# Moving the transposes of y and the sum of z within the step of a pipelined attention and feed-forward kernel

## The reference

```python
normed = rms_norm(x, gamma)
q, k, v = heads of normed @ w_q, normed @ w_kv          # 8 heads of 16
q, k = taylor(q / 4), taylor(k)                         # [1, x, x (x) x / sqrt(2)]
out = (q @ (k^T v)) / max(q . sum(k), 1e-5)
x = layernorm(x + out @ w_out)
h = silu((x @ w1.T) * s1) * ((x @ w2.T) * s2)           # 128 -> 512
h = gelu((h @ h1.T) * sh1)                              # 512 -> 512
h = gelu((h @ h2.T) * sh2)
x = layernorm(x + (h @ w3.T) * s3)                      # 512 -> 128
```

## Time and profile before

| | before |
|---|---|
| median of 3 runs | 554.48 us (554.03 to 554.76) |
| profiled execution | 553.77 us, span 551.7 us |
| busy share of the span | TensorE 97%, VectorE 83%, ScalarE 82%, GpSimd 37% |
| mean granted TensorE clock | 0.996 of full |

### The profile page before, as it was taken

How to read it: one execution, slowest core, us unless ns; L and a number is a source line. 1 busy time by engine, 2 the same in 40 slices (tenths; PEclk the granted TensorE clock), 3 DMA queues, 4 the chain that set the end, 5 groups by cost and what they waited for, 6 DMA issues and landing times.

```text
span 551.7 us, 11595 instructions
## 1 busy us (share of the span) xinstructions
PE 533.3 (97%) x3578; PEld 404.2 (73%) x3578; DVE 457.1 (83%) x966; ACT 454.6 (82%) x941; POOL 202.3 (37%) x280
## 2 busy tenths in 40 slices
PE   6879999999999999999999999999999999999995
PEld 4556868878686887878788787877868687786774
DVE  5888869798797879978797987978889797888674
ACT  3777898988889888888988888898888889787774
POOL 3865334252443423345342533434144353310001
PEclk9999999999999999999999999999999999999998
DMA  8202200201211020121202112110211210010001
GB/s 288 67 23 58 58 21 7 71 21 39 58 38 57 16 55 24 38 57 38 57 0 60 35 38 57 38 57 5 52 38 38 57 38 19 1 33 6 8 13 38
DMA packets 28405, 23.81 MB, mean 43 GB/s; under 512 B 3552, under 2 KB 21472, under 8 KB 28384
## 3 DMA queue, kind: packets, MB, share of 16 engines
q1 hardware_dynamic: 28096, 23.43, 15.9%
q10 hardware_dynamic: 288, 0.10, 0.1%
HBM read 19.31 MB, written 4.22 MB: 43 GB/s over the span
## 4 chain that ended last, share of the span: by engine, by line
PE 88%; DVE 1%; ACT 1%; issue 0%; POOLq 0%; POOL 0%; DVEq 0%
PE fps L524 29%; PE fps L527 29%; PE ring L459 6%; PE ring L437 5%; PE ring L490 5%; PE ring L408 4%; PE ring L499 3%; PE ring L507 2%; PE ring L416 2%; PE fps L569 1%; PE fps L515 1%; PE ring L446 1%; PE ring L470 1%; DVE h L1113 1%; PE ring L477 0%; DVE hid_lo L1119 0%
## 5 line engine op out<-in xcount | busy, mean ns | idle before, releaser
L524 PE MATMUL fps<-hid_hi,w_hi 128*128 128x512 f32 (+1 forms) x584 | 230.6, 396 | 0.0
L527 PE MATMUL fps<-hid_lo,w_hi 128*128 128x512 f32 (+1 forms) x584 | 227.5, 391 | 0.9 <-DVE hid_lo L1127 0.5
L862 ACT ACTIVATE hid_hi<-fps,col 128x512 fp32r<-128x512 f32 x127 | 89.6, 706 | 46.9 <-PE fps L527 46.9
L524 PEld LDWEIGHTS fps<-hid_hi,w_hi 128*128 128x128 f32 x584 | 109.9, 188 | 24.9 <-issue 3.4
L527 PEld LDWEIGHTS fps<-hid_lo,w_hi 128*128 128x128 f32 x584 | 109.9, 188 | 23.4 <-DVE hid_lo L1127 0.9
L1127 DVE TENSOR_TENSOR hid_lo<-fps,hid_hi 128x512 fp32r<-128x512 f32 x127 | 86.1, 687 | 20.5 <-ACT fps L864 19.5
L864 ACT ACTIVATE fps<-fps,col 128x512 f32<-128x512 f32 x127 | 85.9, 676 | 0.0
L1113 DVE SCALAR_TENSOR_TENSOR h<-fps,col,gate_zo 128x512 f32<-128x512 f32 x64 | 47.6, 745 | 41.3 <-ACT gate_zo L849 35.9
L809 ACT ACTIVATE phiT<-ring 128x512 f32<-128x512 f32 x127 | 77.2, 637 | 3.0 <-PE ring L437 1.8
L303 DVE TENSOR_TENSOR phi_k<-phi_k 128x896 f32<-128x896 f32 x64 | 69.3, 1086 | 0.2 <-ACT v_one L792 0.2
L1119 DVE TENSOR_TENSOR hid_lo<-h,hid_hi 128x512 fp32r<-128x512 f32 x64 | 54.7, 855 | 7.9 <-ACT hid_hi L854 6.4
(11 more groups left out here) (141 smaller groups left out, 921.2 us busy)
## 6 DMA issues: line engine op xcount, KB each, us to landing
x_res<-in_x SPq DMA_DIRECT2D x16, 256.0 KB, 3.8
x_nrm<-in_x SPq DMA_DIRECT2D x15, 256.0 KB, 2.8
out<-gate_zo SPq DMA_DIRECT2D x15, 256.0 KB, 2.3
x_cols<-in_xT SPq DMA_DIRECT2D x14, 256.0 KB, 2.6
rn_row<-rn_rows SPq DMA_DIRECT2D x14, 256.0 KB, 4.2
w_raw<-in_h SPq DMA_DIRECT2D x2, 1024.0 KB, 8.8
w_raw<-in_w SPq DMA_DIRECT2D x3, 256.0 KB, 4.4
sel_raw<-in_sel SPq DMA_DIRECT2D x1, 320.0 KB, 5.1
```

The costliest lines, as they stand in the source:

```text
L524: nc.tensor.matmul(out, w[:, o:o + P], hi, start=start, stop=False)
L527: return nc.tensor.matmul(out, w[:, o:o + P], lo, start=False, stop=stop)
L862: nc.scalar.activation(hid[1 - layer][0][:, m, :], fps[:, bank, :], ACT.Gelu, scale=scale)\
```

## The change

`transpose_y` moves from behind `apply_rest` to behind `transpose_rest`, on TensorE. Its output goes to bank 2 of `ring` in place of bank 0 of `fps`, so the entry yT moves from the table FPS to RING and its semaphores with it. `sum_z` is cut in two: the addition of x1, which reads the PSUM bank, goes between gate_mult(1) and gate_lo(0) on VectorE; mean and variance stay behind `normalise` as `var_of_z`. The last step's own form is moved in the text alone. All arithmetic is the same. The change's name also says that the state is done by tiles; the diff has no edit to `state`, and it stands as before.

```diff
--- before.py
+++ after.py
@@ -42,13 +42,13 @@
 
 
 RING = (
-    ("stateT", MIDDLE, 0), ("restT", MIDDLE, 1), ("xT", FRONT, 2), ("acc0", MIDDLE, 0), ("acc1", MIDDLE, 1),
+    ("stateT", MIDDLE, 0), ("restT", MIDDLE, 1), ("xT", FRONT, 2), ("yT", TAIL, 2), ("acc0", MIDDLE, 0), ("acc1", MIDDLE, 1),
     ("kv0", FRONT, 3), ("kv1", FRONT, 2), ("kv2", FRONT, 3), ("kv3", FRONT, 2), ("qT", FRONT, 0), ("out", MIDDLE, 1),
     ("sq0", FRONT, 2), ("sq1", FRONT, 1), ("rest0", FRONT, 3), ("sq2", FRONT, 0), ("sq3", FRONT, 2), ("sq4", FRONT, 1),
     ("rest1", FRONT, 3), ("sq5", FRONT, 0), ("sq6", FRONT, 2), ("state", FRONT, 1), ("sq7", FRONT, 3))
 FPS = (
     ("a0", FFN, 0), ("b0", FFN, 1), ("a1", FFN, 2), ("b1", FFN, 3), ("a2", FFN, 0), ("b2", FFN, 1), ("a3", FFN, 2),
-    ("b3", FFN, 3), ("yT", TAIL, 0), ("two0", FFN, 1), ("two1", FFN, 2), ("two2", FFN, 3), ("two3", FFN, 0),
+    ("b3", FFN, 3), ("two0", FFN, 1), ("two1", FFN, 2), ("two2", FFN, 3), ("two3", FFN, 0),
     ("three0", FFN, 1), ("three1", FFN, 3), ("three2", FFN, 2), ("x1T", MIDDLE, 0), ("three3", FFN, 1), ("y", FFN, 3))
 
 
@@ -564,11 +564,11 @@
             def transpose_y(t):
 
                 pe.wait_ge(f_free[bank_of(FPS, "y")], read(FPS, t - 1, "y"))
-                bank_wait(FPS, f_free, t, "yT")
+                bank_wait(RING, ring_free, t, "yT")
                 for j in range(NT):
-                    mm = nc.tensor.transpose(fps[:, bank_of(FPS, "yT"), j * P:(j + 1) * P], yT[:, j * P:(j + 1) * P],
+                    mm = nc.tensor.transpose(ring[:, bank_of(RING, "yT"), j * P:(j + 1) * P], yT[:, j * P:(j + 1) * P],
                                              ident)
-                mm.then_inc(f_full, 1)
+                mm.then_inc(ring_full, 1)
 
             def last_layers(t, in_full):
 
@@ -630,6 +630,10 @@
                     if middle:
                         transpose_state(t)
                         transpose_rest(t)
+                    if is_step(t, B + 2):
+                        last_transposes()
+                    elif tail:
+                        transpose_y(t)
                     if is_step(t, 0):
                         transpose_x(0)
                     if ffn:
@@ -638,10 +642,6 @@
                     if middle:
                         apply_main(t)
                         apply_rest(t)
-                    if is_step(t, B + 2):
-                        last_transposes()
-                    elif tail:
-                        transpose_y(t)
                     if front:
                         project_kv(t, 0)
                         project_kv(t, 1)
@@ -1078,14 +1078,17 @@
                 nc.vector.tensor_scalar(veps[:, :], mv[:, :, 1], LN_EPS, None, ALU.add).then_inc(veps_ready, 1)
 
             def sum_z(t, par):
-                bank = bank_of(FPS, "yT")
+                bank = bank_of(RING, "yT")
                 if is_positive(t - 3):
                     dve.wait_ge(out_ready, t - 3)
-                dve.wait_ge(f_full, written(FPS, t, "yT"))
+                dve.wait_ge(ring_full, written(RING, t, "yT"))
                 nc.vector.tensor_tensor(z[:, :, :].rearrange("p j d -> p (j d)"),
-                                        x1[par][:, :, :].rearrange("p j d -> p (j d)"), fps[:, bank, :],
-                                        ALU.add).then_inc(f_free[bank], 1)
-                dve.wait_ge(f_free[bank], read(FPS, t, "yT"))
+                                        x1[par][:, :, :].rearrange("p j d -> p (j d)"), ring[:, bank, :],
+                                        ALU.add).then_inc(ring_free[bank], 1)
+
+            def var_of_z(t):
+                bank = bank_of(RING, "yT")
+                dve.wait_ge(ring_free[bank], read(RING, t, "yT"))
                 for j in range(NT):
                     nc.vector.bn_stats(zstats[:, j, :], z[:, j, :])
                 dve.drain()
@@ -1166,6 +1169,8 @@
 
                     gate_mult(t, 0)
                     gate_mult(t, 1)
+                if tail:
+                    sum_z(t, 1 - par)
                 if ffn:
                     gate_lo(t, 0)
                     gate_mult(t, 2)
@@ -1176,7 +1181,7 @@
                 if middle:
                     normalise(t)
                 if tail:
-                    sum_z(t, 1 - par)
+                    var_of_z(t)
                 if front and not is_step(t, B - 1):
                     sum_squares(t + 1)
                 if ffn:
```

## The result

The changed kernel takes 558.56 us (median of 6 runs, 557.96 to 560.78) against 554.62 for the one before (median of 6, measured beside it): ratio 1.0078, 95% interval 1.0062 to 1.0094. That is 3.9 us slower where 1.3 were forecast, and above the range. The profiled execution took 559.12 us for a span of 556.9.

What follows compares the result with a forecast made beforehand. TensorE's stream was taken to bound steps 3 to 16, and VectorE's gates step 17. The transposes' +0.7 us over 14 steps and sum_z's +0.6 in step 17 made +1.3: 555.8 us, range 554.1 to 556.9.

Steps and rivals of the forecast that it cites:

- So there are two regimes: Steps 3 to 16 cost slots in TensorE's stream; in step 17 nothing else covers the gates and TensorE waits for VectorE.
- 0.7 + 0.6: The sum: +0.7 us for the transposes in steps 3 to 16, +0.6 for sum_z in step 17.
- a wait in the gates of every step: Rival: silu(2) or gate_lo slips past its cover, or project_kv(1) waits for sum_z; 559.3 us, chance 0.06.
- The new place of the transposes: Behind transpose_state and transpose_rest on TensorE: four transposes take 0.44 us a step, without a wait.
- The old place: Behind apply_rest: 0.58 us of transposes leave, project_kv's first product exposes 0.20, so 0.38 to 0.39 a step is freed.
- Rival (a): Steps come out even: project_kv's load exposes only 0.14 us; only step 17's +0.6 is left, 555.1 us; chance 0.25.
- (b): Rival, faster: the load of w_qkv behind apply_rest is fetched early and hidden; 553.1 us, chance 0.07.
- The sum of the steps: Transposes' move in steps 3 to 16: 0.44 - 0.39 = +0.05 us a step, 14 steps, +0.7 us.
- The sum of z between the gates: On VectorE, 0.65 us at either place: 0 in steps 3 to 16, where cover absorbs it; not free in step 17.
- Step 17: sum_z ahead of gate_lo(0) delays each later gate by 0.60 to 0.65 us, and TensorE at two0: +0.6 us.

Runs made afterwards that it cites:

- run 2: Kernel before, with 250 instructions more in TensorE's branch that is not taken: 557.57 us (1.0062).
- run 1: Changed kernel, with 8 instructions more in TensorE's branch that is not taken: 555.31 us (1.0021).
- the late sum: In step 17 alone, sum of z in its old place behind the last gate_lo; by itself in the changed kernel: 557.62 us (1.0069).
- run 7: Changed kernel, with 4 instructions more in the branch that is not taken: 555.38 us (1.0022).
- run 5: Changed kernel, with 8 instructions more in the branch not taken and step 17's sum of z in its old place: 555.19 us (1.0021).
- run 11: Changed kernel, with the body that runs directly behind TensorE's branch and step 17's sum of z in its old place: 554.65 us (1.0017).
- run 8: Kernel before, with 226 instructions more in the branch that is not taken: 555.28 us (1.0018).
- run 4: Changed kernel, with the body that runs placed first, directly behind TensorE's branch: 555.64 us (1.0027).
- run 9: Changed kernel, with 2 instructions more in the branch that is not taken: 559.22 us (1.0082).
- Run 10: Kernel before, with the body that runs placed first, directly behind TensorE's branch: 554.54 us (1.0008).
- run 3: Changed kernel, with step 17's sum of z in its old place behind the last gate_lo: 557.62 us (1.0069).

## Why the prediction was wrong

**The step that failed** is "So there are two regimes", and with it the sum "0.7 + 0.6": it has terms for steps 3 to 17 alone, and takes all ahead of step 3 as untouched, because the code that runs there is the same. What runs is the same; where it lies is not. That is worth 1.0062 made in the kernel before (run 2, 3.4 us), and 1.0078 - 1.0021 = 0.0057, 3.2 us, taken off the changed kernel (run 1). By the rows the two profiled executions are 4.2 us apart at the transposes of step 2 (L477 49.31 and 45.07), and their spans are 5.2 apart: in this pair nothing took it back. The medians show less. One wait that can take a part back is TensorE's for GpSimd in step 2, 0.3 to 0.7 us in the four profiles with a stall and 0.6 to 1.4 in the nine without. None of the rivals was this one: "a wait in the gates of every step" gives nearly the measured time, 559.3, by a mechanism that did not happen.

There was a sign of it in the trace of the kernel before. L507's idle time of 1.12 us was put down to VectorE's att, in VectorE's timeline

```profile
30.18 0.71 DVE L1050 STREAM_TRANSPOSE att<-wide 128x512 f32<-128x512 f32 x1
```

but att was ready at 30.89 (30.18 + 0.71) and L507 began at 31.71. The last 0.8 us are the branch's: in the nine profiles with the jump and a record ahead of the edge, L507 begins 1.57 to 1.65 us behind the end of the first transfer of instructions. I read waits only from 60 us on, and so never met a branch.

**The new place of the transposes**: right to 0.01 us. The chain of waits of the changed kernel, step 8, answers to the earlier trace rows:

```profile
243.81 0.22 PE ring L470 x2
244.03 0.11 PE ring L477
244.14 0.44 PE ring L569 x4
...
248.28 1.02 PE ring L499 x8
249.29 0.94 PE ring L408 x6
```

0.44 for the four. **The old place**: project_kv's six products take 0.94 instead of 0.73, 0.21 exposed behind the tiled stage where 0.20 was taken from the load behind the state. Rival (a), that only 0.14 would be, fell, and so did (b). By the Trainium skill (TensorEngine Tiling, Key Properties) a change of tiling mode drains TensorE. The trace agrees that both followers come late, and shows that the price differs with the follower: 0.14 for a float32 transpose, 0.21 for a load of rounded weights.

**The sum of the steps** was mis-sized: the pieces say +0.06 to 0.07 a step, 0.8 to 1.0 in all, but the distances between the groups of transposes grew from a mean of 32.346 to 32.367 us, 0.02 a step. From project_out of step 2 to the first transposes of the last step (L600) it is 486.6 to 486.7 us in the five profiles with the old order (before: 544.73 - 58.01) and 487.5 to 487.6 in the five with the new one (after: 549.93 - 62.35), and 487.1 in the three with the late sum. So 0.5 us is step 17 and 0.4 the steps, where 0.7 was forecast. Why the slots of the other products are together 0.03 to 0.04 us a step shorter stays open.

**The sum of z between the gates**: in full steps free, as said. VectorE's timeline in step 8 answers to the earlier trace rows:

```profile
244.37 0.75 DVE L1116 SCALAR_TENSOR_TENSOR h<-fps,col,gate_zo 128x512 f32<-128x512 f32 x1 [0.31 <-ACT gate_zo L849]
245.04 0.68 DVE L1085 TENSOR_TENSOR gate_zo<-x,ring 128x512 f32<-128x512 f32 x1
245.63 1.18 DVE L1122 TENSOR_TENSOR hid_lo<-h,hid_hi 128x512 fp32r<-128x512 f32 x1
246.74 0.74 DVE L1116 SCALAR_TENSOR_TENSOR h<-fps,col,gate_zo 128x512 f32<-128x512 f32 x1
```

The stretched gate_lo(0) gave back only a part (1.36 to 1.18 us): gate_mult(2) starts 2.37 us behind gate_mult(1), where it was 2.34 (242.26 - 239.92), the idle 0.30 us taking up most of it. No wait of TensorE came of it. **Step 17**: +0.6 forecast, +0.5 by the rows; sum_z's slot is 0.60, and some 0.1 of it filled the gaps in front of gate_lo(0) and gate_mult(2).

**What stays open.** By the rows, a changed kernel without stall is 0.9 us longer, and with the late sum 0.4. The medians of the time give 1.4 and 1.3 (runs 1 and 7) and 1.1 and 0.7 (runs 5 and 11). Each run lists its span beside its time, and this settles a part. In the kernel before, 2.0 us of the time lie outside the span; in run 1 it is 2.4, in run 5 2.2, in run 8 2.7. By the medians of the span alone the difference to the kernel before is 1.25 and 1.2 (runs 1 and 7), 0.75 and 0.8 (runs 5 and 11) and 0.45 (run 8). So the late sum does take off its 0.5 us in run 5 too, and 0.3 of that run's miss lies outside the span. What makes the time outside the span longer isn't in any trace.

Inside the span 0.3 to 0.4 us stay unplaced. The profiles scatter by more than that: in those of runs 4, 5, 7 and 9 the filler matmul ahead of the branch starts at 30.4 to 30.8 us, in the others at 29.3 to 29.8, and the four late ones have a granted clock of 0.71 to 0.74 between 10 and 15 us, where all others have 1.00. This doesn't come with the change: the mean granted clock is 0.995 or less in 26 of the 68 runs of the kernel before and in 21 of the 47 of runs 1, 4, 5, 7 and 11. TensorE's wait for GpSimd in step 2, 0.6 to 1.4 us without a stall, is in single profiles only, and whether it is longer with one kernel than with another they can't say. Run 10, with the order of before, is 0.7 us above the kernel before by its spans, which isn't explained either.

## What to carry to other kernels

Where an engine's program has a branch or two copies of a body, every edit of the first copy moves the second; an edit that adds no work can cost 3 us because a target comes to lie a few instructions ahead of a block's edge. Look for idle time put down to "issue", in the middle of a group of products with no wait in it; ask the view of DMA for transfers of kind `instruction` that end just ahead of where the engine goes on; and test it with a few instructions that are never run before looking for a cause in the change. A comparison of two orders in such a kernel compares code positions as well, and is fair only when both have been shown to be clear of the edge.

## What the runs showed of the hardware

Loading of code: the ten kernels with a jump behind the filler matmul have two transfers of 16 KB of instructions on queue 8 between 28 and 36 us, their starts 3.1 to 3.9 us apart, and the three without the jump have none there. TensorE's first product comes 1.57 to 1.65 us behind the end of the first. Where it has to wait for the second, it goes on 1.3 to 1.5 us behind its end.

Code position, by the count of instructions: a break of 2.6 to 3.1 us on TensorE with the target 3 instructions ahead of the edge (changed kernel, runs 2 and 3), none with the target 1, 3, 5 or 11 behind it, 0.2 us with 27 ahead of it, and about 3.4 us more than the usual wait with 1 ahead (4.46 against 1.1). In the three profiles with a break TensorE is mostly idle from 30 to 35 us (0.7 to 1.6 us busy), 35 to 40 us has a granted clock of 0.50, and the eight products of project_out take 2.2 us in place of 1.1. Placing the body directly behind the branch shortened the way from the filler to the first product by 0.7 us, without a gain in time.
